# Fewer signals from TensorE per unit of a mixture-of-experts stage, and transposes moved ahead of the first product

## What is computed

```python
h = tok(x, ...)                          # patch projection, coordinate/spinor mix, layer norm, output projection
h = h + s4(layernorm(h), ...)            # a state space model, here a length-49 convolution per channel
h = h + ffn(layernorm(h), ...)           # mixture of experts

def ffn(t):                              # t: 3136 tokens x 128
    hs = gelu(einsum('td,nfd->ntf', t, sw1) + sb1)          # 2 shared experts, 512 wide, for all tokens
    shared = einsum('ntf,ndf->td', hs, sw2) + sb2.sum(0)
    cw = top-2 of softmax(t @ gate_w.T + gate_b), else 0
    hr = gelu(einsum('td,efd->etf', t, rw1) + rb1)          # 8 routed experts
    oe = einsum('etf,edf->etd', hr, rw2) + rb2
    return shared + einsum('etd,te->td', oe, cw)            # each token needs only its own two experts
```

## Time and profile before

| | us |
|---|---|
| three executions | 422.87, 419.55, 420.45 |
| their median | 420.45 |
| the profiled execution, its own time | 421.23 |
| its span, from the first instruction to the last | 419.3 |
| PE busy in the span | 351.7 |
| ACT busy | 206.7 |
| DVE busy | 185.0 |
| POOL busy | 174.2 |

### The profile page before, as it was taken

The page is one execution under the profiler, slowest core; times in us unless marked ns, Lnnn a source line. Parts: engine busy times, 40 slices in busy tenths (PEclk is TensorE's granted clock), DMA queues, the critical chain, the costliest instruction groups (busy, mean ns, idle before and its releaser), DMA issues.

```text
span 419.3 us, 7099 instructions
## 1 busy us (share of the span) xinstructions
PE 351.7 (84%) x2476; PEld 291.1 (69%) x2476; DVE 185.0 (44%) x584; ACT 206.7 (49%) x424; POOL 174.2 (42%) x226
## 2 busy tenths in 40 slices
PE   1989989979757996598999999999999999989400
PEld 1657566756646875497788798898898898878300
DVE  2954867478694115918882221121131121121176
ACT  2758568374616323555632453644545554445163
POOL 7071362553212400710002667767767765752100
PEclk9999999989968999557988999999999999999855
DMA  6957459500113420220030144444443543555195
GB/s 177 272 154 189 144 136 301 201 0 1 49 68 116 161 74 0 79 77 1 26 146 13 52 168 147 163 159 164 169 159 140 188 145 110 216 185 164 36 279 158
DMA packets 22172, 54.38 MB, mean 130 GB/s; under 512 B 4553, under 2 KB 10113, under 8 KB 22141
## 3 DMA queue, kind: packets, MB, share of 16 engines
q1 hardware_dynamic: 17789, 46.35, 33.6%
q0 software_dynamic: 3968, 7.41, 6.4%
q10 hardware_dynamic: 384, 0.23, 0.2%
HBM read 28.10 MB, written 6.93 MB: 84 GB/s over the span
## 4 chain that ended last, share of the span: by engine, by line
PE 53%; issue 14%; DVE 13%; DMA 7%; POOL 5%; POOLq 4%; DVEq 2%; ACT 2%; SPq 0%; ACTq 0%
PE bank L1553 12%; PE bank L1530 12%; PE bank L1540 8%; PE bank L1288 3%; DVE dT L859 3%; DMA out<-osb 2%; PE bank L1505 2%; PE bank L1510 2%; PE bank L1511 2%; PE bank L1512 2%; PE bank L1321 2%; DMA Tt<-kpad 2%; PE bank L1588 1%; PE bank L1375 1%; PE bank L1577 1%
## 5 line engine op out<-in xcount | busy, mean ns | idle before, releaser
L636 POOL DMA_INDIRECT xg<-yd,take x56 | 54.5, 974 | 64.0 <-DVE give L1207 47.3
L795 ACT ACTIVATE gf<-bank,wb 128x256 f32<-128x256 f32 (+1 forms) x128 | 51.4, 448 | 52.5 <-PE bank L1530 52.5
L643 POOL DMA_INDIRECT rd<-og,give x56 | 55.2, 986 | 41.4 <-DVE og L1221 28.9
L1553 PE MATMUL bank<-wb,gf 128*128 128x128 f32 x448 | 55.4, 275 | 1.0 <-DVE og L1221 1.0
L1530 PE MATMUL bank<-x,wb 128*128 128x256 f32 (+1 forms) x256 | 54.0, 354 | 2.1 <-issue 1.2
L1553 PEld LDWEIGHTS bank<-wb,gf 128*128 128x128 f32 x448 | 53.2, 192 | 1.5 <-DVE og L1221 1.4
L795 ACT ACTIVATE gf<-bank,vcol 128x392 f32<-128x392 f32 x64 | 35.4, 588 | 36.3 <-PE bank L1512 36.3
L1530 PEld LDWEIGHTS bank<-x,wb 128*128 128x128 f32 x256 | 43.3, 191 | 9.3 <-issue 1.4
L1540 PE MATMUL bank<-gf,ws 128*128 128x392 f32 x128 | 44.8, 492 | 0.0
L1214 DVE COPY x<-bank 128x256 f32<-128x256 f32 (+1 forms) x32 | 12.5, 392 | 65.5 <-PE bank L1588 65.4
L1321 PE MATMUL bank<-patchT,Wp 128*128 128x392 f32 x96 | 37.9, 522 | 0.0
(11 more groups left out here) (268 smaller groups left out, 606.2 us busy)
## 6 DMA issues: line engine op xcount, KB each, us to landing
wb<-tab SPq DMA_DIRECT2D x32, 578.0 KB, 3.2
Xc<-in_x SPq DMA_DIRECT2D x12, 784.0 KB, 6.3
rk<-rd SPq DMA_DIRECT2D x8, 392.0 KB
Tt<-kpad SPq DMA_DIRECT2D x8, 300.1 KB
raw<-in_L_ffn_rw SPq DMA_DIRECT2D x1, 2048.0 KB, 10.1
out<-osb SPq DMA_DIRECT2D x8, 196.0 KB
Tt<-kpad SPq DMA_DIRECT2D x2, 600.2 KB
Tt<-kpad SPq DMA_DIRECT2D x1, 1200.5 KB
```

What stands on the lines that cost most here:

```text
L636: G.indirect_dma_start(out=xg[i % AHEAD][:, t, :], out_offset=None, in_=yd[:, :], in_offset=bass.IndirectOffsetOnAxis(ap=take[:, at:at + 1 ...
L643: G.indirect_dma_start(out=rd[:, :], out_offset=bass.IndirectOffsetOnAxis(ap=give[:, at:at + 1], axis=0), in_=og[i % 2][:, t, :], in_offse ...
L795: nc.scalar.activation(gf[q % 2][:, o, 0:width(q)], bank[o][:, 0:width(q)], ACT.Gelu, bias=bias1(n, o)).then_inc(act_done, 1)
L1553: last = MM(bank[7][:, D * t:D * (t + 1)], gf[q % 2][:, o, 128 * t:128 * (t + 1)], wb[i % WB][:, FO + F + o * D:FO + F + (o + 1) * D], sta ...
```

## The change

PE signals `up_done` once per unit, after the last block, for `up_done`'s four. The transposes of the next routed unit's rows are issued ahead of `up(q + 1)` in place of behind it, and their own signal is gone except for the first unit: who waited for it now waits for the `up_done` of the first product that follows them. All waits count accordingly.

```diff
+        def rows_in(i):
+            return (tin_done, 1) if i == 0 else (up_done, AT[NSH + i - 1] + 1)
...
             def gather(i):
                 if i >= AHEAD:
-                    pool.wait_ge(tin_done, i - AHEAD + 1)
+                    pool.wait_ge(*rows_in(i - AHEAD))
...
             def gelu(q):
                 n = ORDER[q]
+                act.wait_ge(up_done, q + 1)
+                if q >= 2:
+                    act.wait_ge(down_done, q - 1)
                 for o in range(FO):
-                    act.wait_ge(up_done, FO * q + o + 1)
-                    if o == 0 and q >= 2:
-                        act.wait_ge(down_done, q - 1)
                     nc.scalar.activation(gf[q % 2][:, o, 0:width(q)], ...).then_inc(act_done, 1)
...
             def keep_x(i):
-                dve.wait_ge(tin_done, i + 1)
+                dve.wait_ge(*rows_in(i))
                 if i >= 2:
-                    dve.wait_ge(up_done, FO * (AT[NSH + i - 2] + 1))
+                    dve.wait_ge(up_done, AT[NSH + i - 2] + 1)
...
             def up(q):                       # on PE
                 for o in range(FO):
                     ...
-                    last.then_inc(up_done, 1)
+                last.then_inc(up_done, 1)
...
             def transpose_in(i):
...
-                last.then_inc(tin_done, 1)
+                if i == 0:
+                    last.then_inc(tin_done, 1)
...
             for q in range(NU):
...
                 if q == AT[NSH] - 1:
                     transpose_in(0)
+                if routed_at(q + 1) and ORDER[q + 1] - NSH < NB - 1:
+                    transpose_in(ORDER[q + 1] - NSH + 1)
                 if q + 1 < NU:
                     up(q + 1)
                 if q == 0:
                     count_places()
-                if routed_at(q + 1) and ORDER[q + 1] - NSH < NB - 1:
-                    transpose_in(ORDER[q + 1] - NSH + 1)
```

## The result

| | before | changed |
|---|---|---|
| executions timed for this comparison | 17 | 17 |
| median, us | 422.29 | 425.90 |
| lowest to highest, us | 419.22 to 429.77 | 421.62 to 434.33 |
| ratio, with its 95% interval | | 1.0084 (1.0053 to 1.0116) |

The changed kernel is slower by 0.84%, 2.2 to 4.9 us. Measured again later it came out at 1.0124 (1.0057 to 1.0192). The forecast was +1.6 us and 422.0; 425.9 lies above the range of 420.0 to 424.3.

The account below looks back on a forecast made before the run. The prediction took PE's stream to bound the stage of units. Its terms, +0.83 + 0.85 - 0.11 = +1.6 us on a median of 420.45, gave 422.0 us, no measurable change; range 420.0 to 424.3.

Parts of the forecast that it names:

- The signals themselves: In PE's stream of units, removing 175 signals saves nothing: 0 us; faster rival at 415.9 us, chance 0.05.
- ACT waits for the whole first product: In two-tile units gelu starts 1.3 us later, covered by PE's second product and transposes: cost 0, margin 1.1 us or more.
- Between the first two units: The second unit starts some 0.8 us later, absorbed by PE's 1.69 us idle time behind it: cost 0.
- The last shared unit: Ahead of a one-tile routed unit, PE waits 0.6 us for gelu plus 0.24 refill: 0.85 us, bounds 0.4 and 1.0.
- The first routed unit: Transposes now ahead of its first product make PE wait for the second gather: 0.83 us, range 0.7 to 1.1.
- The stop at 374.51: At PE's 1.19 us stop near the end, a one-tile transpose moves into idle time: gain 0.11 us, bounds 0 and 0.11.
- The clock falls in the new hole: Rival: longer PE idle before the first routed unit drops the clock, costing 1.65 us; time 423.6, chance 0.15.
- A late gather: Rival: second gather lands after 5.5 us, PE restarts 3.8 us late and the clock falls; time 426.7, chance 0.1.
- The level: Starting time for the whole kernel: the sum was added to the median of three executions, 420.45, giving 422.0 us.

Follow-up runs that it names:

- e5: Kernel before with 368 more signals on semaphores that nobody awaits, in shared first products and all second products: ratio 0.9972 (0.9895 to 1.0048).
- e1: Kernel before with only the signals changed: one per first product, ACT waiting for all of it, transposes left in place; ratio 1.0079 (1.0047 to 1.0112).
- c4: Changed kernel unaltered, traced a fourth time in one execution: its three stretches of the stage of units sum to 208.6 us.
- c1: Kernel before run again with nothing changed, as a control: ratio 0.9984 (0.9909 to 1.0058).
- f4: Changed kernel with an extra POOL instruction (0.80 us) between the first and second gather: 15.5 us from first gather's issue to first routed second product.
- e3: Changed kernel with the second routed unit's transposes put back behind the first routed unit's first product, with their own signal: ratio 1.0116 (1.0068 to 1.0164).
- e4: Changed kernel with the second routed unit's transposes put back and the last shared unit signalling block by block: ratio 1.0078, again 1.0012.
- f1: Kernel before with seven shared units ahead of the first routed one in place of six: ratio 1.0101 (1.0025 to 1.0177).
- f3: Changed kernel with seven shared units ahead of the first routed one and the last shared unit signalling block by block: ratio 1.0063 (1.0019 to 1.0108).
- e2: Kernel before with only the order changed: transposes ahead of the first product, all signals kept; ratio 1.0048 (1.0011 to 1.0084).
- f2: Changed kernel with seven shared units ahead of the first routed one in place of six: ratio 1.0070 (1.0029 to 1.0112).

## Why the prediction was wrong

The forecast was +1.6 us; the medians differ by 3.6. The mean of the four sums of the changed kernel is 207.1, 2.6 us above before's 204.4 and 204.5. That is 0.6%, inside the interval of the ratio. By the prediction's own steps:

- *The signals themselves, 0*: right. The rule of the Trainium skill (TensorE: Matmul & The Clock Gate, The cost: per-tile semaphore tail) would, by an estimate from its figure, have made e5 9.7 us slower (368 times its 26.3 ns); it was not. That rule is about packed tiles, and no run here has such tiles.
- *ACT waits for the whole first product, 0 in the dense part*: right, no wait in 45 units. Between the first two units the wait was 0.8 us, and PE's idle time behind it took it up, as said.
- *The last shared unit, 0.85*: 0.7 in the changed kernel (`up` 1.76 against 1.06), 0.8 in e1. Right place, a little too high. Gelu's four blocks took 2.02 us and not the 2.19 that stood in the sum: that length was PE's pace (last section).
- *The first routed unit, 0.83*: right cause, and 0.7 to 0.8 where PE comes late, as in the trace that I read (B 13.1 against 12.3). Where PE comes early the new idle time is 3.0 us and not 1.8. I took one trace as the kernel's constant.
- *The stop at 374.51, -0.11*: 0.12 by PE's stop, 1.07 us against 1.19.
- *The clock falls in the new hole*: **the step that failed**. I had it as a rival with a chance of 0.15 and 1.65 us, and with nothing in the sum. Its premise was that PE's idle time grows "from about 0.9 to 1.8 us". At 1.7 us the clock stayed up, in three traces of three. But in two of the changed kernel's four traces the idle time was 3.0 us, and it fell. That cost 1.4 us of B in the trace shown and 2.8 in c4, where the half clock lasted twice as long (3.2 and 6.6 us of it are in the stretches shown): 1.1 us in the mean of four traces, nearly as much as the two holes, and it belonged in the sum. The 1.65 us themselves were of the right size for one such fall.
- *Time lost ahead of the gathers*, not in the prediction: in the trace shown A is 1.3 us longer than in the other three. Before's kernel takes such a delay back (c1 and e5: A longer by 0.8, B shorter by 0.7). In the changed one the second gather's landing sets when `up` starts, and nothing is taken back. That is 0.3 us in the mean. With 0.8 for the first hole, 0.55 for C and 1.1 for the clock it makes 2.7, against the 2.6 found.
- *A late gather, 0.1*: did not happen; the landing there was 2.5 us in all four traces of the changed kernel.
- *The level*: 422.0 stood on a median of three, 420.45. Over 17 executions before's median is 422.29. That alone moves the forecast by 1.8 us, more than the 1.6 by which the range missed. (The top of the range, 424.3, is also 0.15 below what its own terms give, 421.23 + 1.57 + 1.65.) Three executions spread over 3.3 us were not treated as what they are: a kernel whose time varies by 2.5% (419.22 to 429.77 us).

What is shown: both holes, in the traces, by undoing each. That the fall belongs to the first hole is shown by counts (three of six against none of ten), by the four traces in which PE comes as early but the transposes stand behind, and by f4. Why PE comes early or late, that is why the clock falls 36 us into the stage in some executions and not in others, was not looked for. What stays open besides: the timing does not confirm the undoing. e1, e3 and e4 measured 1.008 to 1.012 with sums at most 0.9 us above before's, and e4 did not repeat it. The likeliest reading is that an interval from a dozen executions is too narrow for these kernels, because the clock falls at other places ahead of the units in each execution: in the sixteen traces the first unit starts at 188.2 to 197.7 us. No run here settles it.

## What to carry to other kernels

Fewer signals are no gain where the next matmul starts as soon behind a signalling one as behind a silent one; what a coarser signal moves is the start of whoever waits, so look for the few places without cover (the first unit, a short unit behind a long one), not at the mean. Work that is hoisted in front of a critical product brings its own wait along: check its first use, where the buffers ahead are not yet full. And an added idle stretch of TensorE is measured in several traces, with the engine coming early and coming late, and the clock's fall behind it is priced into the sum by its likely share, not kept as a remote rival.

## What the runs showed of the hardware that I had not expected

- Gelu's four blocks take 1.57 us in the changed kernel (order in time, first routed unit) and 1.77 us before; for a shared unit 2.02 and 2.17 to 2.19. It looks as if the single wait made ACT faster, but one gelu is as long as before, 474 ns (groups by line and shape: before from 235 to 385 us, changed from 245 to 400 us).

```profile
247.11 1.57 ACT L799 ACTIVATE gf<-bank,wb 128x256 f32<-128x256 f32 x4 [8.09 <-PE bank L1534]
```

```profile
L795 ACT ACTIVATE gf<-bank,wb 128x256 f32<-128x256 f32 x93 | 41.0, 474 | 40.1 <-PE bank L1530 40.1
L799 ACT ACTIVATE gf<-bank,wb 128x256 f32<-128x256 f32 x96 | 37.6, 474 | 56.5 <-PE bank L1534 56.5
```

  What differs is the spacing: before, the gelus start 0.43 us apart, which is PE's pace for a block (1.73 us for four), in the changed kernel 0.37 us apart. In the one-tile units, where a block takes PE only 0.22 us, the four take 1.14 us in both kernels. So a wait ahead of each gelu shows no cost of its own, and a row's length can hold the pace of another engine.

- The time outside the span (an execution's own time less its span) has a median of 1.8 to 2.1 us in before, the changed kernel, e4, e5, f1 and f3, but of 2.5 to 2.8 in e1, e2, e3 and f2 (2.6 in f4's one execution). Single executions cross over: e2 and e4 both go from 1.8 to 3.0. The changed kernel has 1.9, so it is no part of the result, but it is 0.7 to 0.9 us of what e1, e2 and e3 measured. The cause was not looked for.
